# The last stage's feed-forward on rounded high and low halves, three products for each plain fp32 one, with the second matrix chunk by chunk

## The chip, the cores and the metric

The kernel runs on one core of a Trainium2 chip. The core has TensorE (PE, matrix products into PSUM), VectorE (DVE), ScalarE (ACT), GpSimd (POOL) and SyncE (SP, which here issues every DMA), each with its own instruction queue; they meet at semaphores. The metric is the device time of one execution in microseconds (us).

## What is computed

Only the part that the change touches is shown; `src` is the normalised input plus the mixture-of-experts attention that the earlier stages have made, and a second small causal attention is added at the end.

```python
src = _ln(src + src2, ln1_g, ln1_b)                 # src2: the attention with experts
src2 = jax.nn.relu(src @ W1 + b1) @ W2 + b2         # W1 (256, 1024), W2 (1024, 256)
ffn = _ln(src + src2, ln2_g, ln2_b)
out = x + attn(xn) @ WO + ffn                       # x (8, 512, 256), float32
```

## The kernel before

The batch has B = 8 sequences of 512 tokens with D = 256 features. A first stage normalises and turns all of them. A long loop over 64 steps (8 pairs of heads times 8 sequences, PAIRS = 64) makes projections, attention and the output mix of the experts; its steps are laid out by hand in eight slots for each engine (PE_FILL, ACT_FILL, DVE_FILL, POOL_FILL). Steps come in kinds: INNER in the loop, LAST for the 64th, TAIL for what trails behind it. In LAST and TAIL what remains of a step is mainly the mix: for each of 8 experts e VectorE makes uf (L1239), ScalarE rounds it to u_h (L1041), GpSimd makes the rest u_l = uf - u_h ("UL", L573), and TensorE multiplies wo_h by u_h and u_l and wo_l by u_h ("J", `mix`, L799).

This way of splitting an fp32 factor in a rounded high half and a low half (tiles of type float32r) and taking three products is used in the whole loop: GpSimd makes the halves of the weights from a staging tile (`halves`, L511 to L515: one add, a wait, one subtract), `split_wv` and `split_wo` once for each pair of heads.

The last stage works on one sequence b after another and is plain fp32. On TensorE (L908 to L922) one repetition is:

- `turn_y(b+1)`: 8 transposes of the next sequence (L880);
- `hidden(b, f)` for f = 0 to 7 (FC = 8 chunks of 128 hidden features): 2 matmuls of 512 columns each into bank f0 or f1 in turn (L897);
- `turn_s1(b+1)`: 8 transposes of the next normalised sequence (L888);
- `rows_of("z")`: hidden features times W2, 32 matmuls of 256 columns, after all of `hidden` (L905);
- `rows_of("w")`: 8 matmuls of 256 columns for the other attention's output (L905).

ScalarE takes each hidden chunk out of PSUM with one Relu (L1079), copies the turned s1 (L1068), and takes square roots for the norms (`roots`, L932). VectorE, in this order for each b: `first_norm(b+1)` (statistics L1102 and L1105, var L1107, the wait for the root, L1109 to L1114, L1116, then two multiplications over 128x1024, L1281 and L1282), `with_bias` (L1288), aT (L1300, L1301), the sum with z (L1306), the second norm (again L1102 to L1116), and the residual (L1312). GpSimd does three operations of 128x1024 for each sequence (L635, L637, L644), the last of which makes the tile that is stored. SyncE loads both matrices in one piece each (L477, L478) after the last of the mix's inputs is made, and TensorE waits for both (`c_in`, L910).

In a norm the root of `first_norm(b+1)` is taken by ScalarE at hidden chunk f = 4 (L1074), and that of the second norm of b right after the last chunk and the copies of s1 (L1082).

Of the kernel before, what the change touches and what calls it, by code (L numbers as in the profile page):

```python
# [6 lines left out]
B, S, D = 8, 512, 256  # L7
# [125 lines left out]
def build(nc, x, wqk, wv, wo, w_out, w1, w2, b1, rows, ident, ident_h, mask, rope, rank, out):  # L133
# [11 lines left out]
    with ExitStack() as ctx:  # L145
# [83 lines left out]
        s1T = probs[:, 1]  # L229
# [8 lines left out]
        den_all, rden_all = st[:, 1].rearrange("q (g s) -> q g s", g=2), st[:, 0, 0:S]  # L238
# [69 lines left out]
        s1_ready = sem("s1_ready")  # L308
        acc_ready = sem("acc_ready")
# [18 lines left out]
        def _(sp):  # L328
# [143 lines left out]
            for j in range(2):  # L472
                sp.wait_ge(wo_split[j], HP)
# [30 lines left out]
        def _(pool):  # L504
# [17 lines left out]
            def split_wv(p, j):  # L522
                pool.wait_ge(st_in[j], 32 * p + 16)
                halves(wv_h[:, j], wv_l[:, j], st[:, j].rearrange("q (k n) -> q k n", k=KC),
                       zero_hb[:, None, :].to_broadcast([NP, KC, S]), 5 * p + 2 + j, wv_split[j])

            def split_wo(p, j):
# [4 lines left out]
                       zero_hb[:, None, :].to_broadcast([NP, 2, S]), 5 * p + 4 + j, wo_split[j])  # L532
# [14 lines left out]
            def body(kind, it, p=None, wv_next=False, wo_now=False):  # L547
# [82 lines left out]
            body(TAIL, PAIRS - 1)  # L630

            pool.wait_ge(c_in, 64)
            for b in range(B):
                pool.wait_ge(acc_ready, b + 1)
                nc.gpsimd.tensor_tensor(acc, acc, rows_sb[:, 2:3, :].to_broadcast([NP, TT, D]), ALU.mult).then_inc(fin_step, 1)  # L635
                pool.wait_ge(fin_step, 2 * b + 1)
                nc.gpsimd.tensor_tensor(acc, acc, rows_sb[:, 3:4, :].to_broadcast([NP, TT, D]), ALU.add).then_inc(fin_step, 1)  # L637
                pool.wait_ge(fin_step, 2 * b + 2)
                pool.wait_ge(resid_ready, b + 1)
                if b > 0:  # L640
                    pool.wait_ge(out_stored, 16 * b)
                else:
                    pool.wait_ge(rden_out, 16)
                nc.gpsimd.tensor_tensor(fin, acc, x_c[b % 2], ALU.add).then_inc(fin_ready, 1)  # L644

        @block.tensor
        def _(pe):
# [243 lines left out]
            def hidden(b, f):  # L891
                if f == 0:
                    for k in range(KC):
                        pe.wait_ge(c_free[f"w{k}"], s1T_at(b) + 1)
                o = c_bank(f"f{f % 2}", b * (FC // 2) + f // 2)
# [14 lines left out]
            pe.wait_ge(c_in, 64)  # L910
# [14 lines left out]
        def _(act):  # L925
# [139 lines left out]
            def s1_out(b):  # L1065
                for k in range(KC):
                    act.wait_ge(c_full[f"w{k}"], s1T_at(b) + 1)
                    nc.scalar.activation(s1T[:, k, :], cbank[f"w{k}"][:], ACT.Copy).then_inc(c_free[f"w{k}"], 1)  # L1068
# [294 lines left out]
```

## Time and profile before

| | |
|---|---|
| median of 3 runs | 3404.74 us (3403.65 to 3405.85) |
| span of the profiled execution | 3401.4 us |
| its first to last instruction, clock granted to TensorE | 0.995 |
| TensorE, matmuls | 3233.1 us busy, 95% |
| VectorE | 2439.7 us, 72% |
| ScalarE | 1961.5 us, 58% |
| GpSimd | 1441.9 us, 42% |
| the last stage (from 3112 us on) | about 289 us of the span |

The span runs from the first to the last instruction; the time of a run is 3.3 us longer (3404.74 less 3401.4). The page cuts the span in 40 slices of 85 us, so the last stage is its last three and a half digits. In a row of the timeline the first number is the start from the span's start, the second how long the instruction ran in us, then come engine, line, operation, the tile written and those read; the bracket at the end says how long the engine had been idle and what released it. A matmul's record is longer than the distance to the next one, since they are pipelined: what one costs is read from start to start. A plain fp32 matmul leaves two records.

### The profile page before, as it was taken

To read this page: it belongs to the slowest core of one execution; us is meant where nothing else is said; L and a number is where in the kernel's file an instruction comes from. 1 tells how busy PE (TensorE), PEld (TensorE's weight loads), DVE (VectorE), ACT (ScalarE), POOL (GpSimd) and SP (SyncE) were. 2 spreads that over 40 slices of the span, in tenths; PEclk is the share of its full clock that TensorE was granted. 3 is DMA by queue.
4 is the path that set the end of the run, shared out by engine and by line. 5 is a ranking of instruction groups with operands and counts; after the bars stand their busy time and mean duration, and the time that the engine had idled before them with its cause. 6 is when DMAs were issued, how large, how long until landed. Compare 5 with 4: busy or idle time off the path is not lost.

```text
span 3401.4 us, 64468 instructions
## 1 busy us (share of the span) xinstructions
PE 3233.1 (95%) x18240; PEld 2378.9 (70%) x18240; DVE 2439.7 (72%) x4708; ACT 1961.5 (58%) x4509; POOL 1441.9 (42%) x1215
## 2 busy tenths in 40 slices
PE   1699999999999999999999999999999999997998
PEld 1577777777777777777777777777777777775765
DVE  6577777777777777777777777777777777775554
ACT  2466666656666666666666666666666666664121
POOL 4144355445443454345543554434534543442212
PEclk9999999999999999999999999999999999999999
DMA  5223333334233333233233332333332433333221
GB/s 165 76 71 87 95 90 85 77 76 109 76 84 87 84 98 81 75 100 96 69 87 76 96 98 77 76 104 81 84 87 68 114 81 75 84 75 110 72 83 62
DMA packets 115937, 295.18 MB, mean 87 GB/s; under 512 B 33856, under 2 KB 54592, under 8 KB 99264
## 3 DMA queue, kind: packets, MB, share of 16 engines
q1 hardware_dynamic: 115904, 294.78, 32.9%
q8 instruction: 15, 0.25, 0.0%
q14 instruction: 18, 0.15, 0.0%
HBM read 262.74 MB, written 31.98 MB: 87 GB/s over the span
## 4 chain that ended last, share of the span: by engine, by line
PE 85%; issue 6%; DVE 5%; ACT 3%; DMA 1%; POOL 0%; ACTq 0%; SPq 0%; DVEq 0%; POOLq 0%
PE bank L673 27%; PE bank L799 22%; PE bank L718 9%; PE bank L773 7%; PE bank L688 5%; PE bank L905 4%; PE bank L897 3%; PE bank L693 3%; PE bank L745 2%; PE bank L754 2%; ACT probs L957 2%; DVE uf L1239 1%; DVE oo L1232 1%; PE bank L694 1%; ACT pt_e L977 1%
## 5 line engine op out<-in xcount | busy, mean ns | idle before, releaser
L573 POOL TENSOR_TENSOR u_l<-uf,u_h 128x512 fp32r<-128x512 f32 x512 | 716.1, 1409 | 722.6 <-ACT u_h L1041 722.4
L1136 DVE TENSOR_REDUCE nmax<-bank 128x1 f32<-128x512 f32 (+3 forms) x1024 | 551.8, 579 | 305.0 <-PE bank L688 297.8
L673 PE MATMUL bank<-wv_h,xx 128*128 128x512 f32 x2048 | 755.0, 410 | 7.1 <-DVE vm L1157 7.1
L957 ACT ACTIVATE probs<-bank,nmax 128x512 f32<-128x512 f32 (+3 forms) x1024 | 590.7, 610 | 253.2 <-DVE nmax L1136 253.1
L1041 ACT ACTIVATE u_h<-uf 128x512 fp32r<-128x512 f32 x512 | 321.7, 632 | 696.9 <-DVE uf L1239 683.6
L673 PEld LDWEIGHTS bank<-wv_h,xx 128*128 128x128 f32 x2048 | 386.0, 188 | 155.8 <-issue 59.6
L718 PEld LDWEIGHTS bank<-ident_sb,probs 128*128 128x128 f32 x3328 | 388.3, 141 | 106.4 <-issue 51.3
L718 PE MATMUL bank<-ident_sb,probs 128*128 128x128 f32 x3328 | 451.3, 274 | 1.6 <-ACT stackT L1032 0.9
L569 POOL TENSOR_TENSOR v_sb<-v_next,zero_hb 128x512 f32<-128x512 f32 x64 | 74.2, 1160 | 891.9 <-PE bank L773 877.4
L799 PE MATMUL bank<-u_h,wo_h 128*128 128x512 f32 x1024 | 427.1, 417 | 5.0 <-ACT u_h L1041 3.2
L1239 DVE TENSOR_TENSOR uf<-oo,go 128x512 f32<-128x512 f32 x512 | 416.2, 823 | 8.8 <-POOL u_l L573 6.6
L799 PE MATMUL bank<-u_h,wo_l 128*128 128x512 f32 x1024 | 405.9, 396 | 0.0
L799 PE MATMUL bank<-u_l,wo_h 128*128 128x512 f32 x1024 | 405.0, 396 | 0.0
L673 PE MATMUL bank<-wv_l,xx 128*128 128x512 f32 x1024 | 404.8, 395 | 0.0
L1157 DVE TENSOR_TENSOR vm<-bank,gv 128x512 f32<-128x512 f32 x512 | 348.4, 681 | 41.6 <-PE bank L673 41.5
L1159 DVE TENSOR_REDUCE v_next<-vm 128x64 f32<-128x512 f32 x512 | 351.3, 686 | 17.6
L673 PE MATMUL bank<-wq_h,xx 128*128 128x384 f32 x1024 | 280.4, 344 | 12.8 <-DMA xx<-xs_d 12.7
L977 ACT ACTIVATE pt_e<-bank 128x512 f32<-128x512 f32 x512 | 276.1, 594 | 5.1 <-PE bank L718 0.5
L799 PEld LDWEIGHTS bank<-u_h,wo_h 128*128 128x128 f32 x1024 | 192.4, 188 | 66.5 <-issue 24.4
L773 PE MATMUL bank<-pt_e,v_sb 128*64 128x512 f32 x1024 | 233.8, 598 | 0.0
L1191 DVE TENSOR_SCALAR vm<-raw 128x128 f32<-128x128 f32 x64 | 14.5, 227 | 296.6 <-ACT raw L992 296.6
L799 PEld LDWEIGHTS bank<-u_h,wo_l 128*128 128x128 f32 x1024 | 192.5, 188 | 46.5
(141 smaller groups left out, 5164.2 us busy)
## 6 DMA issues: line engine op xcount, KB each, us to landing
go<-go_d SPq DMA_DIRECT2D x256, 512.0 KB, 6.5
xx<-xs_d SPq DMA_DIRECT2D x128, 512.0 KB, 3.5
oo<-scale_d SPq DMA_DIRECT2D x128, 128.0 KB, 2.9
a_d<-a_out SPq DMA_DIRECT2D x128, 128.0 KB, 2.3
pt_c<-in_x SPq DMA_DIRECT2D x16, 512.0 KB, 4.7
st<-in_wv SPq DMA_DIRECT2D x16, 512.0 KB, 5.8
st<-in_wo SPq DMA_DIRECT2D x16, 512.0 KB, 7.2
go_d<-go_turned SPq DMA_DIRECT2D x256, 8.0 KB
```

Of the source, the lines that this page charges most:

```text
L573: nc.gpsimd.tensor_tensor(u_l[:, e % 2], uf[:, e % 2], u_h.bitcast(f32)[:, e % 2], ALU.subtract).then_inc(ul_done, 1)
L673: last = nc.tensor.matmul(out, lhs, rhs, start=n == 1, stop=n == 3 * len(chunks))
L718: mm = nc.tensor.transpose(o[:, c * NP:(c + 1) * NP], probs[:, s % 2, j, c * NP:(c + 1) * NP], ident_sb[:])
L773: mm = nc.tensor.matmul(o[j * P:(j + 1) * P, :], v_sb[:, k, j, :], pt_e[:, j, k, :], start=k == 0, stop=k == TT - 1)
L799: mm = nc.tensor.matmul(ybank[i][:], w[:, e, c], u[:, e % 2], start=e == 0 and k == 0, stop=e == E - 1 and k == 2, skip_group_check=True)
L957: nc.scalar.activation(probs[:, s % 2, j, 0:w], sbank[j][:, 0:w], ACT.Exp, bias=nmax[:, 2 * s + j:2 * s + j + 1], **kw).then_inc(exp_done, 1)
L977: nc.scalar.activation(dst[:, j, 0:m, qt * NP:(qt + 1) * NP], tbank[j][:, 0:m * NP].rearrange("q (c m) -> q c m", m=NP), ACT.Copy).then_in ...
L1041: nc.scalar.activation(u_h[:, i % 2], uf[:, i % 2], ACT.Copy).then_inc(uh_done, 1)
L1136: nc.vector.tensor_reduce(nmax[:, 2 * s + j:2 * s + j + 1], sbank[j][:, 0:w], AX.X, ALU.max, negate=True).then_inc(nmax_ready, 1)
L1157: nc.vector.tensor_tensor(m, o[:].rearrange("q (c e) -> q c e", e=E), g, ALU.mult).then_inc(free, 1)
L1159: nc.vector.tensor_reduce(v_next[:, t, j, :], m, AX.X, ALU.add).then_inc(v_ready, 1)
L1239: nc.vector.tensor_tensor(uf[:, i % 2], oo[:, 0], go[:, i], ALU.mult).then_inc(u_ready, 1)
```

## The change

In the last stage both matrices, the turned s1 and the hidden features are kept as rounded high half and low half, and each fp32 product becomes three (high by high, high by low, low by high). In particular:

- The weights use the buffers of the loop: W1 goes through the staging tile into wv_h and wv_l, W2 into wo_h and wo_l. SyncE issues W1's two loads ahead of step LAST and W2's two behind it; GpSimd splits W1 inside LAST (after slots 2 and 4) and W2 behind TAIL.
- `hidden(b, f)` is 6 matmuls of 512 columns. `expand(b, f)` takes the place of `rows_of("z")`: 12 matmuls of 256 columns for one chunk f, which follow two chunks behind `hidden`; the last three come after `turn_s1(b+1)`.
- ScalarE takes each chunk out twice (plain, and rounded), then waits for its own second write before a small copy sets the bank free. `roots` for the second norm of the sequence before moves to chunk f = 1 of the next sequence.
- GpSimd makes the low half of each chunk (`hidden_rest`), and its three closing operations of the sequence before are placed behind chunks 2, 3 and 5.
- VectorE makes the low half of s1 (`s1_low`, two operations of 128x512 out of PSUM), behind aT.

```diff
-        w1_sb = go[:, 0:4].rearrange("q (k a) s -> q k (a s)", k=KC)
-        w2_sb = go[:, 4:8].rearrange("q a (c n) -> q (a c) n", n=D)
-        hT = pe8
+        hidden_f = [pe8[:, i] for i in range(4)]
+        hidden_h = [u_h[:, 0], u_h[:, 1], q_h[:], k_h[:]]
+        hidden_l = [u_l[:, 0], u_l[:, 1], q_l[:], k_l[:]]
...
+            for j in range(2):
+                sp.wait_ge(wo_split[j], HP)
+                sp.dma_start(st[:, j].rearrange("q (k n) -> q k n", k=KC), w1[:, :, j * F // 2:(j + 1) * F // 2]).then_inc(st_in[j], 16)
             body(HP - 1, B - 1, LAST, before=(HP - 1, B - 2))
+            for j in range(2):
+                sp.wait_ge(wv_split[j], HP + 1)
+                sp.dma_start(st[:, j].rearrange("q (a n) -> q a n", n=D), w2[:, j * FC // 2:(j + 1) * FC // 2, :]).then_inc(st_in[j], 16)
...
-            sp.wait_ge(u_ready, E * PAIRS)
-            sp.dma_start(w1_sb, w1).then_inc(c_in, 16)
-            sp.dma_start(w2_sb, w2).then_inc(c_in, 16)
...
+                    if kind == LAST and s in (2, 4):
+                        j = s // 2 - 1
+                        pool.wait_ge(w_full, w_at(INNER, PAIRS - 2, ("V", 5 + 2 * j))[2] + 1)
+                        split_wv(HP, j, 1)
...
+            for j in range(2):
+                pool.wait_ge(o_done, (PAIRS - 1) * E + (j + 1) * E // 2)
+                split_wo(HP, j, 3)
+
+            def hidden_rest(b, f):
+                n = b * FC + f
+                i = n % 4
+                pool.wait_ge(hidden_ready, n + 1)
+                if n >= 4:
+                    pool.wait_ge(z_step, n - 3)
+                nc.gpsimd.tensor_tensor(hidden_l[i], hidden_f[i], hidden_h[i].bitcast(f32), ALU.subtract).then_inc(hidden_low, 1)
...
+                for f in range(FC):
+                    hidden_rest(b, f)
+                    if b > 0 and f in (2, 3, 5):
+                        finish(b - 1, (2, 3, 5).index(f))
...
                 o = c_bank(f"f{f % 2}", b * (FC // 2) + f // 2)
-                for k in range(KC):
-                    mm = nc.tensor.matmul(o[:], w1_sb[:, k, f * NP:(f + 1) * NP], s1T[:, k, :], start=k == 0, stop=k == KC - 1)
-                mm.then_inc(c_full[f"f{f % 2}"], 1)
+                j, c = f // (FC // 2), slice(f % (FC // 2) * NP, (f % (FC // 2) + 1) * NP)
+                three(o[:], [(wv_h[:, j, k, c], wv_l[:, j, k, c], s1T[:, 0, k, :], s1T[:, 1, k, :]) for k in range(KC)]).then_inc(c_full[f"f{f % 2}"], 1)
+
+            def expand(b, f):
...
+                pe.wait_ge(hidden_low, n + 1)
+                hi, lo = hidden_h[n % 4], hidden_l[n % 4]
+                for t in range(TT):
+                    o = cbank[f"z{t // 2}"][:, (t % 2) * D:(t % 2 + 1) * D]
+                    c = slice(t * NP, (t + 1) * NP)
+                    for i, (lhs, w) in enumerate(((hi[:, c], wo_h), (hi[:, c], wo_l), (lo[:, c], wo_h))):
+                        mm = nc.tensor.matmul(o, lhs, w[:, f, :], start=f == 0 and i == 0 and t % 2 == 0, stop=f == FC - 1 and i == 2,
...
                 for f in range(FC):
                     hidden(b, f)
+                    if f > 1 and f < FC - 1:
+                        expand(b, f - 2)
                 if b + 1 < B:
                     turn_s1(b + 1)
-                for i in range(2):
-                    pe.wait_ge(c_free[f"f{i}"], (b + 1) * (FC // 2))
-                rows_of("z", b, hT, w2_sb, FC)
+                for f in range(FC - 3, FC):
+                    expand(b, f)
...
+                nc.scalar.activation(hidden_f[i], o[:], ACT.Relu, bias=b1_sb[:, f:f + 1])
+                nc.scalar.activation(hidden_h[i], o[:], ACT.Relu, bias=b1_sb[:, f:f + 1]).then_inc(hidden_ready, 1)
+                act.wait_ge(hidden_ready, n + 1)
+                nc.scalar.activation(primer[:, 1:2], ident_sb[0:1, 0:1], ACT.Copy).then_inc(c_free[f"f{f % 2}"], 1)
...
+                    if f == 1 and b > 0:
+                        roots(B + 2 * b)
                     if f == FC // 2 and b + 1 < B:
                         roots(B + 2 * b + 1)
...
+            def s1_low(b):
+                for k in range(KC):
+                    dve.wait_ge(s1h_ready, KC * b + k + 1)
+                    nc.vector.tensor_tensor(s1T[:, 1, k, :], cbank[f"w{k}"][:], s1T[:, 0, k, :].bitcast(f32), ALU.subtract).then_inc(c_free[f"w{k}"], 1)
...
+                if b + 1 < B:
+                    s1_low(b + 1)
                 if b > 0:
                     dve.wait_ge(fin_ready, b)
```

## Rows read from the trace of the kernel before

**Rows 1.** The page: TensorE's busy tenths in 40 slices.

```profile
PE   1699999999999999999999999999999999997998
```

**Rows 2.** Chain of waits in order of time, one repetition of the last stage.

```profile
3290.86 0.87 PE bank L880 x8
3291.74 13.73 PE bank L897 x32
...
3306.37 17.43 PE bank L905 x80
3323.80 0.87 PE bank L880 x8
```

**Rows 3.** The same repetition: length, then busy us of PE, PEld, DVE, ACT, POOL; clock.

```profile
3290.90:3323.80 32.90, 32.90 (x130) 22.84 (x129) 19.16 (x50) 6.77 (x12) 7.06 (x3) 1.00 0.25 80
```

**Rows 4.** Timeline of TensorE, split matmuls of 512 and 384 columns.

```profile
1501.62 0.39 PE L673 MATMUL bank<-wv_h,xx 128*128 128x512 f32 x1
1501.85 0.39 PE L673 MATMUL bank<-wv_l,xx 128*128 128x512 f32 x1
...
1521.33 0.33 PE L673 MATMUL bank<-wq_l,xx 128*128 128x384 f32 x1
...
1521.85 0.33 PE L673 MATMUL bank<-wq_l,xx 128*128 128x384 f32 x1
```

**Rows 5.** Timeline of TensorE's weight loads, the first two after an idle time.

```profile
3100.36 0.19 PEld L799 LDWEIGHTS bank<-u_h,wo_h 128*128 128x128 f32 x1 [0.71 <-issue]
3100.47 0.19 PEld L799 LDWEIGHTS bank<-u_l,wo_h 128*128 128x128 f32 x1
```

**Rows 6.** Timeline of ScalarE, first stage: the first reading of two banks in turn.

```profile
23.38 0.60 ACT L941 ACTIVATE y_sb<-bank 128x512 f32<-128x512 f32 x1 [7.36 <-PE bank L659]
...
24.75 0.57 ACT L941 ACTIVATE y_sb<-bank 128x512 f32<-128x512 f32 x1
```

**Rows 7.** Timelines of VectorE and GpSimd, small VectorE operations beside GpSimd's.

```profile
27.57 2.04 DVE L1112 TENSOR_TENSOR root<-root,rstd 128x4 f32<-128x4 f32 x1
...
27.48 2.12 POOL L513 TENSOR_TENSOR wv_h<-st,zero_hb 128x1024 fp32r<-128x1024 f32 x1
29.68 2.34 POOL L515 TENSOR_TENSOR wv_l<-st,wv_h 128x1024 fp32r<-128x1024 f32 x1
...
3257.94 0.16 DVE L1112 TENSOR_TENSOR root<-root,rstd 128x4 f32<-128x4 f32 x1
...
3263.13 1.69 DVE L1107 TENSOR_SCALAR var<-mv 128x4 f32<-128x4 f32 x1
...
3262.44 2.35 POOL L637 TENSOR_TENSOR pt_c<-pt_c,raw 128x1024 f32<-128x1024 f32 x1
```

**Rows 8.** Timeline of VectorE, landmarks of one repetition of the last stage.

```profile
3254.51 0.69 DVE L1306 TENSOR_TENSOR pt_c<-bank,pt_c 128x512 f32<-128x512 f32 x1 [6.03 <-PE bank L905]
...
3261.26 1.42 DVE L1102 BATCH_NORM_STATS2 stats<-bank 128x6 f32<-128x256 f32 x4
...
3266.51 0.18 DVE L1109 RECIPROCAL rstd<-root 128x4 f32<-128x4 f32 x1 [1.70 <-ACT root L932]
...
3274.45 1.22 DVE L1301 TENSOR_TENSOR uf<-uf,oo 128x1024 f32<-128x1024 f32 x1
```

**Rows 9.** Groups by line and form, GpSimd: a low half of 128x512 (mean ns second).

```profile
L537 POOL TENSOR_TENSOR q_l<-y_sb,q_h 128x512 fp32r<-128x512 f32 x4 | 5.1, 1265 | 27.6 <-ACT primer L945 27.6
```

**Rows 10.** Timelines: GpSimd in steps LAST and TAIL, VectorE behind TAIL.

```profile
3069.85 2.70 POOL L573 TENSOR_TENSOR u_l<-uf,u_h 128x512 fp32r<-128x512 f32 x2 [3.17 <-ACT u_h L1041]
3075.03 2.52 POOL L573 TENSOR_TENSOR u_l<-uf,u_h 128x512 fp32r<-128x512 f32 x2 [2.48 <-ACT u_h L1041]
...
3082.62 1.30 POOL L573 TENSOR_TENSOR u_l<-uf,u_h 128x512 fp32r<-128x512 f32 x1 [2.48 <-ACT u_h L1041]
...
3106.72 1.29 POOL L573 TENSOR_TENSOR u_l<-uf,u_h 128x512 fp32r<-128x512 f32 x1 [0.70 <-ACT u_h L1041]
...
3111.05 0.55 DVE L1292 TENSOR_TENSOR st<-st 128x384 f32<-128x384 f32 x1
```

More of the change, by code:

```diff
@@ L308, in build @@
         s1_ready = sem("s1_ready")
+        s1h_ready = sem("s1h_ready")
+        hidden_ready = sem("hidden_ready")
+        hidden_low = sem("hidden_low")
+        z_step = sem("z_step")
         acc_ready = sem("acc_ready")
@@ L531, in split_wo @@
                        st[:, j].rearrange("q (a n) -> q a n", a=2),
-                       zero_hb[:, None, :].to_broadcast([NP, 2, S]), 5 * p + 4 + j, wo_split[j])
+                       zero_hb[:, None, :].to_broadcast([NP, 2, S]), 5 * p + step + j, wo_split[j])
             def split_x(b):
@@ new lines, in hidden_rest, with finish @@
+            def hidden_rest(b, f):
[5 more added lines that the diff above has]
+                nc.gpsimd.tensor_tensor(hidden_l[i], hidden_f[i], hidden_h[i].bitcast(f32), ALU.subtract).then_inc(hidden_low, 1)
+            def finish(b, step):
+                if step == 0:
+                    pool.wait_ge(acc_ready, b + 1)
+                    nc.gpsimd.tensor_tensor(acc, acc, rows_sb[:, 2:3, :].to_broadcast([NP, TT, D]), ALU.mult).then_inc(fin_step, 1)
+                elif step == 1:
+                    pool.wait_ge(fin_step, 2 * b + 1)
+                    nc.gpsimd.tensor_tensor(acc, acc, rows_sb[:, 3:4, :].to_broadcast([NP, TT, D]), ALU.add).then_inc(fin_step, 1)
+                else:
+                    pool.wait_ge(fin_step, 2 * b + 2)
+                    pool.wait_ge(resid_ready, b + 1)
+                    if b > 0:
+                        pool.wait_ge(out_stored, 16 * b)
+                    nc.gpsimd.tensor_tensor(fin, acc, x_c[b % 2], ALU.add).then_inc(fin_ready, 1)
@@ L646, in _ @@
+            pool.wait_ge(c_in, 32)
+            for b in range(B):
+                for f in range(FC):
+                    hidden_rest(b, f)
+                    if b > 0 and f in (2, 3, 5):
+                        finish(b - 1, (2, 3, 5).index(f))
+            for step in range(3):
+                finish(B - 1, step)
         @block.tensor
@@ L894, in hidden @@
                         pe.wait_ge(c_free[f"w{k}"], s1T_at(b) + 1)
+                    if b == 0:
+                        for j in range(2):
+                            pe.wait_ge(wv_split[j], HP + 1)
                 o = c_bank(f"f{f % 2}", b * (FC // 2) + f // 2)
-                for k in range(KC):
-                    mm = nc.tensor.matmul(o[:], w1_sb[:, k, f * NP:(f + 1) * NP], s1T[:, k, :], start=k == 0, stop=k == KC - 1)
-                mm.then_inc(c_full[f"f{f % 2}"], 1)
+                j, c = f // (FC // 2), slice(f % (FC // 2) * NP, (f % (FC // 2) + 1) * NP)
+                three(o[:], [(wv_h[:, j, k, c], wv_l[:, j, k, c], s1T[:, 0, k, :], s1T[:, 1, k, :]) for k in range(KC)]).then_inc(c_full[f"f{f % 2}"], 1)
+            def expand(b, f):
+                if f == 0:
+                    c_bank("z0", b)
+                    c_bank("z1", b)
+                if b == 0 and f % (FC // 2) == 0:
+                    pe.wait_ge(wo_split[f // (FC // 2)], HP + 1)
+                n = b * FC + f
+                pe.wait_ge(hidden_low, n + 1)
[5 more added lines that the diff above has]
+                        mm = nc.tensor.matmul(o, lhs, w[:, f, :], start=f == 0 and i == 0 and t % 2 == 0, stop=f == FC - 1 and i == 2,
+                                              skip_group_check=True)
+                    if f == FC - 1 and t == 1:
+                        mm.then_inc(c_full["z0"], 1)
+                mm.then_inc(z_step, 1)
             def rows_of(name, at, lhs, w, chunks):
@@ L909, in _ @@
             turn_s1(0)
-            pe.wait_ge(c_in, 64)
+            pe.wait_ge(c_in, 32)
             for b in range(B):
@@ L1073, in _ @@
                 for f in range(FC):
+                    if f == 1 and b > 0:
+                        roots(B + 2 * b)
                     if f == FC // 2 and b + 1 < B:
                         roots(B + 2 * b + 1)
-                    if f == 0 and b > 0:
-                        act.wait_ge(c_full["z1"], b)
-                    act.wait_ge(c_full[f"f{f % 2}"], b * (FC // 2) + f // 2 + 1)
-                    nc.scalar.activation(hT[:, f, :], cbank[f"f{f % 2}"][:], ACT.Relu, bias=b1_sb[:, f:f + 1]).then_inc(c_free[f"f{f % 2}"], 1)
+                    hidden_out(b, f)
                 if b + 1 < B:
                     s1_out(b + 1)
-                roots(B + 2 * b + (2 if b + 1 < B else 1))
+            roots(B + 2 * B - 1)
         @block.vector
@@ L1294, in _ @@
             first_norm(0, B)
+            s1_low(0)
             for b in range(B):
@@ L1304, in _ @@
                 for i in range(2):
-                    dve.wait_ge(c_full[f"z{i}"], b + 1)
+                    if i == 0:
+                        dve.wait_ge(c_full["z0"], b + 1)
+                    else:
+                        dve.wait_ge(z_step, (b + 1) * FC)
                     made(nc.vector.tensor_tensor(acc[:, 2 * i:2 * i + 2, :], cbank[f"z{i}"][:].rearrange("q (t d) -> q t d", t=2), s1[b % 2][:, 2 * i:2 * i + 2, :], ALU.add))
```

34 lines of the change are left out of this document (14 added, 20 removed).

## Prediction

> **What bounds the kernel now.** I read the page first: TensorE is busy nine tenths or more in nearly every slice, most of the last stage included [rows 1]. Then the chain of waits in order of time, for the stage that changes: it stays on TensorE without a gap, and the pattern repeats every 3323.80 - 3290.86 = 32.94 us: 0.87 for `turn_y`, 13.73 for `hidden`, 0.90 for `turn_s1` (what is left up to 3306.37), 17.43 for z and w together [rows 2]. The same stretch by windows shows TensorE full, at a granted clock of 1.00, and VectorE 19.2, ScalarE 6.8, GpSimd 7.1 of 32.9 us [rows 3]. So the plain fp32 products are the bound now, and TensorE work taken away counts until another engine ends last. The reader should look at how far the others are from it, and at what they wait for; the busy sums alone mislead here.
>
> **TensorE's side.** Removed: 16 hidden matmuls (13.73 us, 0.858 each) and 32 of z. The 17.43 us are 40 matmuls of 256 columns, 0.436 each with the change of banks; z's 32 are 13.9 and w's 8 are 3.5. Added for each sequence:
>
> - 48 split matmuls of 512 columns. The loop has the same kind: start to start 1501.85 - 1501.62 = 0.23 [rows 4]; 48 x 0.233 = 11.2.
> - 96 split matmuls of 256 columns. The trace has no such form. Three of 384 columns take 1521.85 - 1521.33 = 0.52, 0.174 each [rows 4]. The straight line through 512 and 384 gives 0.115 at 256. A weight load could hold them up: its record is 0.19 long, but at the head of a chain, where nothing else is in the way, the second load starts 3100.47 - 3100.36 = 0.11 behind the first [rows 5], so loads can follow at 0.11. Bounds: 0.11 and the whole record, 0.19. I take 0.117, by the line, which is just above the pace of the loads: 96 x 0.117 = 11.2.
>
> With the turns (0.87 and 0.9) and w (3.5) TensorE needs 27.7, plus 0.3 at `hidden(2)`, which waits for ScalarE to free bank f0 (below): 28.0, that is 4.9 less than now. If TensorE stayed the bound, that would be some 37 us over the stage.
>
> **What ends last instead.** The change gives the others work and, above all, order.
>
> ScalarE: two readings and a small copy for each chunk. The first stage has this pattern, two readings of a bank, a wait, a small copy, and takes 24.75 - 23.38 = 1.37 for the whole [rows 6]; some 1.4 here. TensorE spends 1.4 on a chunk, 2.8 with `expand`. That fits, but the bank of chunk 0 is free only about 3.1 + 0.9 into the repetition, hence the 0.3.
>
> GpSimd: 8 low halves at 1.27 [rows 9] are 10.2, and the three closing operations of about 2.4 are 7.1 [rows 3]: 17.3 where it had 7.1. All closing operations and six of the halves fall between about 8 and 23 us of a repetition, so it works there almost without a break.
>
> VectorE: beside a GpSimd operation its small operations on SBUF don't run. L1112, 0.16 alone, took 2.04 and ended at 29.61, where GpSimd's L513 ends at 29.60; L1107, as small, took 1.69 and ended at 3264.82, GpSimd's L637 at 3264.79 [rows 7]. GpSimd's next operation starts in between, so a chain of such operations loses one GpSimd operation at each link. Operations with an input in PSUM show no such delay.
>
> Now one repetition, from `turn_y` at 0. The pieces of VectorE's chain add up to its landmarks: from the sum with z to the next statistics 6.75, of which 1.9 for statistics and var, 0.3 for the root, 0.9 for L1109 to L1114, 1.3 for L1116, 1.3 for the residual; from L1109 to the end of L1301 9.2, a wait of 0.3 in it [rows 8].
>
> - Root of the second norm of the sequence before. Its var is ready at about 0.3, but ScalarE takes the root only at chunk 1, behind chunk 0: hidden(0) ends at 2.3, drained 2.5, two readings and copy to 3.9, root 4.1. VectorE stands for 3.8. Before, the root was taken at once.
> - L1109 to L1114, 0.9 alone, with two waits for low halves (0.6 and 1.0): 6.8. Four L1116, 1.3: 8.1 (sum ready for GpSimd). Residual, 1.3: 9.4.
> - `first_norm` of the next sequence: statistics 1.9, var with 0.5 of wait, 12.0; root 12.2.
> - L1109 to L1114: behind a closing operation 1.7, behind two low halves 1.1 and 0.8: 16.9. Four L1116 from PSUM 1.9: 18.9. L1281 and L1282 (1.22 each) in turn with low halves, 1.0 of wait: 22.4, s1 is ready.
> - TensorE came to `turn_s1` at 0.87 + 0.3 + 11.2 + 7.0 (5 of the 8 expands) = 19.4 and waits 3.1. From 22.5: turn 0.9, three expands 4.2, w 3.5: 31.1 to 31.2. aT and s1_low (about 5 us of VectorE) lie beside the turn and the expands, and end with them.
>
> So a repetition is 31.2, not 28.0: VectorE's chain with two roots and the waits for GpSimd takes 3.1 of the 4.9 back. Over the stage: six repetitions at -1.75 are -10.5; the first has no closing operations and no second norm before it, so it keeps the gain of TensorE but pays s1_low ahead of `hidden` (0.9): -3.9; the last has no `first_norm`, but is held up by GpSimd's queue for about 2: -3.5. Behind the last z the chain (sum, norm, three GpSimd operations, store) is the same. Sum -17.9.
>
> On this a rule of the Trainium skill bears, page "SBUF — State Buffer", section "Who interferes with whom": a VectorE instruction with two SBUF inputs, or in a two-port mode, contends with a GpSimd instruction that reads SBUF, and whichever issued second blocks in full until the other is done. The rows agree for L1112 and L1107. The page speaks against this change, for it gives GpSimd 10 us more in the very window of the norms; without it the sum would be that of the first rival. The page adds that tensor_scalar can be in such a mode too; for L1116 on SBUF that is the second rival.
>
> **Ahead of the stage.** W1's split, 2.12 + 2.34 with a gap of 0.08 for each half [rows 7], goes into step LAST on GpSimd's queue. Queued behind it are the low halves of u, for which TensorE's mix waits. First half: starts when the fourth u_l is done, 3072.55, and runs to 3077.1; the fifth u_l started at 3075.03 [rows 10], so the mix is 2.1 to 2.5 late. Second half: after the sixth, now at 3079.7, to 3084.3; the seventh then ends at 3085.6 and the eighth at 3086.9, which ended at 3082.62 + 1.30 = 3083.9 [rows 10]. So I take the mixes there as 3.3 late (3.0 by the eighth, the rest for TensorE's turn on the seventh), and I see nothing behind them in LAST or TAIL with slack to give that back. W2's split, 9.1 us behind TAIL's last u_l (3106.72 + 1.29 = 3108.0), covers VectorE's L1292 at 3111.05 [rows 10], two SBUF inputs, which waits for the second operation to end, 1.5; the reciprocal, the norm and the turn hang on it. It is done before the first chunk's low half is due. Sum +4.8. Bounds: 2 (LAST absorbs most) and 8 (another wait in the norm).
>
> The loads: W1's two stand ahead of LAST's, W2's two behind its, and they wait for splits done long before or at 3084.3; what SyncE has queued behind them (rows, w_out, the last of the causal attention, x, the denominators) is wanted after 3108.0 only. GpSimd waits for W2 behind TAIL, over 20 us later. The two loads of 1 MB behind the last mix go away; TensorE's wait for them was over before its first hidden chunk, which waited for the norm. I cost both at nothing; if a load of 0.5 MB came late, it would be 6 us once.
>
> **Sum.** -17.9 + 4.8 = -13.1. Profiled span 3401.4 - 13.1 = 3388.3; with the 3.3 around it, 3391.6, say 3392. The median of before is 3404.74, which is 3401.4 + 3.3, so span and time move together.
>
> **The rivals.**
>
> - TensorE stays the bound. For it: VectorE's own work is only about 21 us of a repetition, and a slightly different phase of GpSimd's operations would spare several waits. Against it: the root at chunk 1 and the rows of L1112 and L1107. Then 28.0 for a repetition, stage -37, sum -32: 3372.
> - GpSimd holds VectorE up further: L1116 on SBUF waits as well, four in each second norm. Nothing in the trace shows it beside GpSimd; its 0.32 us from start to start for 256 elements is the pace of an operation that isn't in a fast mode. Then 32.2 for a repetition, -1.0 less for each of seven: -6, with the upper bound ahead of the stage -2: 3399 to 3403.
> - Slower: the weight load is the pace of the 256-column matmuls. 96 weight loads for each sequence are twice those of z before, and each serves half the columns of one in `hidden`. At the record's 0.19 `expand` takes 18.2, a repetition 35.1, the stage +17 and all +22: 3427. It decides from about 0.16 on, where a repetition with the costs ahead of the stage comes to what it was. The 0.11 between the first two loads of a chain speaks against it.
> - The change doesn't do what it says, the split products run as slow as plain ones. That would be hundreds of us; 0.23 for 512 columns in the loop excludes it as good as surely.
>
> **How the numbers follow.** Forecast 0.50 (3384 to 3399), TensorE-bound 0.17, held up further 0.22, weight loads 0.06, others 0.05. A measurement of this kernel can tell about 0.2%, 6.8 us, from no change: faster means under 3398, slower over 3411.5. Faster: 0.45 of the forecast, 0.17, 0.06 of the third case: 0.68. Slower: 0.06, 0.02 of the third, 0.03 of the others: 0.11. Same: the rest, 0.21. The range reaches from the first rival's 3371 to the upper bound of the second, 3406; what is left out is under 0.2.
>
> **What would show it.** In the profile after: matmuls of `expand` 0.117 apart; a wait of TensorE's `turn_s1` (L888's successor) for VectorE's L1282 of about 3 us in each repetition; repetitions of 31.2; VectorE's small operations at 0.6 to 1.8 us beside GpSimd's; GpSimd near full in the middle of a repetition; ScalarE's root of the second norm some 4 us behind its var; TensorE 3.3 us late at the end of LAST. Wrong would make it: a repetition of 28 without the wait; expands over 0.13 apart; or a TensorE idle for so long that its clock falls.

## The result and the profile after

| | before | after |
|---|---|---|
| median | 3405.13 us (3403.65 to 3406.82, 5 runs) | 3418.23 us (3417.27 to 3420.49, 5 runs) |
| span of the profiled execution | 3401.4 us | 3416.4 us |
| granted clock, whole span | 0.995 | 0.988 |
| GpSimd busy | 1441.9 us | 1545.9 us |

The ratio is 1.004, with a 95% interval from 1.0027 to 1.0053: the kernel became 13 us slower, where 13 us faster was forecast. The predicted range (3371 to 3406) does not hold the time.

The page of the kernel after, TensorE's busy tenths and its clock, shows where: only the last digits differ from [rows 1].

```profile
PE   1699999999999999999999999999999999997887
...
PEclk9999999999999999999999999999999999999988
```

The chain of waits of one repetition of the last stage (start, us, what), the counterpart of [rows 2]. In the changed file L909 is `turn_y`, L702 the three products of `hidden`, L1130 the rounded reading of ScalarE, L983 the root, L1174 to L1177 the old L1111 to L1114, L1179 the old L1116, L1344 and L1345 the old L1281 and L1282, L917 `turn_s1`, L944 `expand`, L955 w.

```profile
3230.82 0.87 PE bank L909 x8
3231.70 1.40 PE bank L702 x6
...
3233.81 0.59 ACT u_h L1130
...
3234.97 0.82 DVE root L1174
...
3236.01 1.26 DVE root L1176
...
3244.10 1.89 DVE root L1174
...
3246.01 1.22 DVE root L1175
3247.25 1.23 DVE root L1176
3248.51 2.31 DVE rstd L1177
3250.85 1.90 DVE probs L1179 x4
...
3254.35 1.24 DVE probs L1345
...
3255.63 1.97 PE bank L917 x8
3257.60 6.04 PE bank L944 x36
3263.64 3.45 PE bank L955 x16
3267.10 0.87 PE bank L909 x8
```

The repetition takes 3267.10 - 3230.82 = 36.28 us; the six of this kind take 36.2, 35.3, 36.3, 35.3, 36.3 and 35.3, on average 35.8, against 32.94 before and 31.2 forecast. The chain is on TensorE only at the two ends. Between them it is mostly on VectorE, at operations on 128x4 elements that need 0.16 to 0.18 us when alone and take 0.8 to 2.3 us here.

The same repetition by windows (length, then busy us of PE, PEld, DVE, ACT, POOL; granted clock), the counterpart of [rows 3]:

```profile
3230.82:3267.10 36.28, 30.77 (x179) 27.52 (x177) 27.81 (x52) 12.91 (x28) 17.22 (x11) 0.91 0.22 73
3250.00:3255.00 5.00, 0.34 (x2) 0.00 (x0) 4.88 (x9) 1.47 (x3) 3.23 (x3) 0.96 0.62 194
3255.00:3260.00 5.00, 4.37 (x21) 4.37 (x22) 4.93 (x6) 1.20 (x2) 0.00 (x0) 0.50 0.06 19
```

TensorE stands nearly still from 3250 to 3255, and when it starts again, the granted clock is 0.50, that is 1.2 GHz instead of 2.4. So the wait is paid twice: once as a wait, and once as `turn_s1` at 1.97 us instead of 0.87 and 36 matmuls of `expand` at 6.04 us.

The two profiled spans differ by 15.0 us, the medians by 13.1; what lies outside the span is 1.8 us in this profiled execution and 3.3 in that of before. Where the 15.0 us are, from matching starts in the two chains:

| stretch | before | after | difference | forecast |
|---|---|---|---|---|
| up to the attention of step LAST | 3058.1 | 3056.6 | -1.5 | 0 |
| LAST, attention to attention | 29.4 | 35.3 | +5.9 | +3.3 |
| TAIL, up to the old L1292 | 23.7 | 23.7 | 0.0 | 0 |
| from there to the first `turn_s1` | 11.5 | 12.9 | +1.4 | +1.5 |
| first repetition | 36.5 | 30.9 | -5.6 | -3.9 |
| six repetitions | 197.6 | 214.7 | +17.1 | -10.5 |
| last repetition | 28.7 | 25.6 | -3.1 | -3.5 |
| behind the last z | 16.0 | 16.7 | +0.7 | 0 |

The first row is not the change's: over the profiles of this study the attention of LAST starts anywhere from 3054.9 to 3061.6 us. The six repetitions are the miss, 27.6 us against their forecast.

### The profile page after: what moved, and what is told of

It is laid out like the page before. It is cut to its first block, busy times and chain, and to the rows that moved or that the text cites. A ratio compares the mean times of both kernels' runs of the same rounds, so it can differ in the third digit from the quotient of the medians.

```text
span 3416.4 us, 65572 instructions
## 1 busy us (share of the span) xinstructions
PE 3209.8 (94%) x18624; PEld 2410.1 (71%) x18624; DVE 2509.8 (73%) x4724; ACT 2010.9 (59%) x4637; POOL 1545.9 (45%) x1287
## 4 chain that ended last, share of the span: by engine, by line
PE 80%; DVE 9%; issue 6%; ACT 3%; POOL 1%; DMA 1%; ACTq 0%; SPq 0%; DVEq 0%; POOLq 0%
PE bank L702 28%; PE bank L828 21%; PE bank L747 9%; PE bank L802 7%; PE bank L717 5%; PE bank L722 3%; PE bank L774 2%; PE bank L783 2%; DVE uf L1302 2%; ACT probs L1008 2%; PE bank L944 1%; DVE oo L1295 1%; PE bank L723 1%; DVE pt_c L1179 1%; PE bank L955 1%
## 5 line engine op out<-in xcount | busy, mean ns | idle before, releaser
L702 PE MATMUL bank<-wv_h,xx 128*128 128x512 f32 x2048 | 754.8, 410 | 7.1 <-DVE vm L1220 7.1
L702 PEld LDWEIGHTS bank<-wv_h,xx 128*128 128x128 f32 x2048 | 386.2, 189 | 155.3 <-issue 59.6
L702 PE MATMUL bank<-wv_l,xx 128*128 128x512 f32 x1024 | 404.4, 395 | 0.0
L702 PE MATMUL bank<-wq_h,xx 128*128 128x384 f32 x1024 | 279.8, 344 | 11.7 <-DMA xx<-xs_d 11.7
L828 PEld LDWEIGHTS bank<-u_h,wo_h 128*128 128x128 f32 x1024 | 192.7, 188 | 70.5 <-issue 25.6
```

Source lines behind the costliest of these rows:

```text
L702: last = nc.tensor.matmul(out, lhs, rhs, start=n == 1, stop=n == 3 * len(chunks))
L828: mm = nc.tensor.matmul(ybank[i][:], w[:, e, c], u[:, e % 2], start=e == 0 and k == 0, stop=e == E - 1 and k == 2, skip_group_check=True)
```

## The experiments

**The two theories at the outset.** After reading the trace of the kernel after, I held that the middle of a repetition is a chain of small VectorE operations, each held until the GpSimd operation beside it ends, and that the wait which this gives TensorE also costs clock. The timelines of the two engines (start, length, engine, line, operation, tiles) show the pairs:

```profile
3244.10 1.87 DVE L1174 TENSOR_TENSOR root<-var,rstd 128x4 f32<-128x4 f32 x1
3246.01 1.21 DVE L1175 TENSOR_TENSOR root<-root,rstd 128x4 f32<-128x4 f32 x1
3247.25 1.22 DVE L1176 TENSOR_SCALAR root<-root 128x4 f32<-128x4 f32 x1
3248.51 2.30 DVE L1177 TENSOR_TENSOR rstd<-rstd,root 128x4 f32<-128x4 f32 x1
...
3243.53 2.42 POOL L658 TENSOR_TENSOR pt_c<-pt_c,raw 128x1024 f32<-128x1024 f32 x1
3245.91 2.54 POOL L650 TENSOR_TENSOR u_l<-pt_e,u_h 128x512 fp32r<-128x512 f32 x2
3248.40 2.39 POOL L664 TENSOR_TENSOR st<-pt_c 128x1024 f32<-128x1024 f32 x1
```

L1174 ends at 3245.97, GpSimd's L658 at 3245.95; L1175 ends at 3247.22, in the middle of the two low halves (3247.18); L1176 at 3248.47, where the second low half ends (3248.45); L1177 at 3250.81, L664 at 3250.79. Four operations that need 0.7 us take 6.6. The rivals to it: the late root, the clock by itself, and the work ahead of the stage.

**e1: the root one chunk earlier.** ScalarE takes the root of the second norm ahead of chunk 0 of the next sequence; in the kernel after it takes it ahead of chunk 1, so behind chunk 0.

```diff
-                    if f == 1 and b > 0:
+                    if f == 0 and b > 0:
                         roots(B + 2 * b)
```

> One edit of the changed kernel: ScalarE takes the root of the second norm ahead of chunk 0 of the next sequence, not behind it. Theory A (VectorE's chain of two norms sets when s1 is ready, and the late root is 3.4 us of it): VectorE gets this root at about 0.6 us of a repetition, not 3.9; s1 is ready at about 22.4, not 24.8; TensorE waits some 3 us ahead of the turn, its granted clock doesn't fall, and a repetition takes about 31.2 where it took 35.8 on average. The whole is 25 to 30 us faster than the changed kernel, about 3390. Rival B (GpSimd's operations alone set VectorE's pace; it would have waited for them anyway): s1 comes at 24 or later, TensorE still waits over 4.5 us and goes cold, at most 5 us gained. Rival C (the loss sits ahead of the stage): no change.

Measured: 3398.54 us (10 runs), ratio 0.9982 (0.9972 to 0.9991), some 20 us under the kernel after, less than the 25 to 30 expected: the waits are shorter, but the clock still fell in three of the six repetitions. The `turn_y`s are 32.7, 32.5, 32.7, 31.2 and 31.2 us apart, where 31.2 was expected for all. In windows two successive repetitions stand beside each other, and the difference between them is the clock:

```profile
3224.45:3257.14 32.69, 29.70 (x179) 26.49 (x177) 27.30 (x53) 13.02 (x28) 19.11 (x11) 0.95 0.25 81
3257.14:3288.33 31.19, 28.20 (x179) 25.00 (x177) 26.78 (x51) 12.82 (x27) 19.11 (x11) 1.00 0.26 85
```

The place of one 0.2 us operation of ScalarE is worth 20 us. But s1 is ready 22.3 us into the repetition (22.4 expected), TensorE still waits 2.78 us for L1345, and the small operations of `first_norm` are still held (L1175 1.20, L1176 2.33, L1177 1.21). The timeline of VectorE shows a second wait in front of them:

```profile
3267.13 0.18 DVE L1172 RECIPROCAL rstd<-root 128x4 f32<-128x4 f32 x1 [3.64 <-ACT root L983]
...
3268.96 2.33 DVE L1176 TENSOR_SCALAR root<-root 128x4 f32<-128x4 f32 x1
```

The root of `first_norm` is still taken ahead of chunk 4, and VectorE, now earlier, stands 3.64 us for it, where it stood 0.27 in the kernel after. So about half of what the early root of the second norm gives is lost at the other root: var is ready 6.3 us into the repetition instead of 12.8, its root is used at 10.0 instead of 13.1. In e6 below this wait is still 1.79 us; no run moves that root.

**e2: without two of the three closing operations.** GpSimd's multiplication by ln2_g and addition of ln2_b are left out, so that the output lacks them; the last closing operation, the sum with x, stays behind chunk 5.

```diff
-                if step == 0:
-                    pool.wait_ge(acc_ready, b + 1)
-                    nc.gpsimd.tensor_tensor(acc, acc, rows_sb[:, 2:3, :].to_broadcast([NP, TT, D]), ALU.mult).then_inc(fin_step, 1)
-                elif step == 1:
-                    pool.wait_ge(fin_step, 2 * b + 1)
-                    nc.gpsimd.tensor_tensor(acc, acc, rows_sb[:, 3:4, :].to_broadcast([NP, TT, D]), ALU.add).then_inc(fin_step, 1)
```

> One edit of the changed kernel: GpSimd's first two closing operations of each sequence (times ln2_g, plus ln2_b, 128x1024 each) are left out, so the output lacks them. Theory A with the shared port as I read it (VectorE's small operations on SBUF wait for whole GpSimd operations, and those behind a closing operation lose 1.7 to 2.3 us each): L1114's counterpart ends at about 14, not 20, of a repetition, s1 is ready at about 21.2, a repetition is some 31, no cold clock; with one closing operation less at the end as well (two of 2.3 behind the last norm), 35 us faster than the changed kernel. Rival (VectorE's chain is long by itself, the waits for GpSimd would only move to the low halves): s1 at 24 or later, a repetition over 34, only the 5 us at the end gained.

Measured: 3385.29 us, ratio 0.9943 (0.9927 to 0.996), 33 us under the kernel after where 35 were expected. 4.7 us of the gain on the kernel after are those two operations behind the last sequence, where nothing hides them (2.34 and 2.33 in its chain); the rest is in the repetitions, now 30.9 us. The chain of waits of one shows the first norm's operations free (compare the four above):

```profile
3236.78 0.19 DVE rstd L1166
3236.99 0.17 DVE root L1168
3237.18 0.17 DVE root L1169
3237.38 0.18 DVE root L1170
3237.58 0.17 DVE rstd L1171
```

s1 is ready 21.1 us into the repetition (21.2 expected). The root is still ahead of chunk 1 here, as in the kernel after. So holding by GpSimd is a cause by itself.

**e3: TensorE kept busy while it waits.** 24 matmuls whose result is overwritten stand ahead of the wait of `turn_s1`.

```diff
             def turn_s1(b):
...
+                if b > 0:
+                    o = c_bank("w0", s1T_at(b))
+                    for i in range(24):
+                        nc.tensor.matmul(o[:], wv_h[:, 0, 0, 0:NP], wv_h[:, 0, 0, :], start=True, stop=True)
```

> One edit of the changed kernel: TensorE runs 24 matmuls of 512 columns (about 5.5 us) whose result is overwritten, ahead of its wait for s1, in each repetition but the first. Theory A (the wait of 5.7 us is VectorE's; on top of it TensorE's clock falls to 1.2 GHz and the turn and the first expands behind it cost 2 to 3 us more): s1 is ready at the same 24.8, the turn takes 0.9 instead of 1.97 and the 36 matmuls of expand 4.3 instead of 5.1 to 6.1; a repetition is 33.5, about 13 us faster in all. Rival B (those matmuls are slow for another reason, such as contention with the copies of s1): they stay at 5 to 6 us, no gain, or a loss if the added matmuls outlast the wait.

Measured: 3415.54 us (3410.99 to 3417.02), ratio 1.003 (1.0017 to 1.0042), against 1.004 (1.0027 to 1.0053) for the kernel after: the intervals overlap, and the gain of 2.7 us between medians is not resolved; 13 had been expected. The profiled execution is the fastest of the six (3410.99), so its span shows more than the median does. What a repetition does can be read in it all the same. The chain of waits of one repetition:

```profile
3251.35 5.44 PE bank L916 x24
3256.78 1.01 PE bank L921 x8
3257.80 4.31 PE bank L948 x36
```

And the window behind the wait, for which the kernel after had a clock of 0.50, now has 1.00:

```profile
3255.00:3260.00 5.00, 5.00 (x36) 4.42 (x36) 4.90 (x6) 1.09 (x2) 0.00 (x0) 1.00 0.28 91
```

The turn takes 1.01 instead of 1.97, the 36 matmuls of `expand` 4.31 instead of 6.04, and repetitions are 33.7 instead of 35.8 us. The six gain 12.3 us; the first, in which TensorE had not waited, pays 5.4 for the added matmuls. That makes -6.9; with the 0.4 us that the stage starts earlier in this profile it is the difference between the spans, 3409.1 - 3416.4 = -7.3. s1 is ready at the same 24.8. So the clock is worth 2.1 us of a repetition, and the chain on VectorE the rest: with a full clock and the same chain a repetition is still longer than before.

**e4: W1 split later.** Both halves of W1 are split behind slot 7 of LAST instead of slots 2 and 4.

```diff
-                    if kind == LAST and s in (2, 4):
-                        j = s // 2 - 1
-                        pool.wait_ge(w_full, w_at(INNER, PAIRS - 2, ("V", 5 + 2 * j))[2] + 1)
-                        split_wv(HP, j, 1)
+                    if kind == LAST and s == SLOTS - 1:
+                        for j in range(2):
+                            pool.wait_ge(w_full, w_at(INNER, PAIRS - 2, ("V", 5 + 2 * j))[2] + 1)
+                            split_wv(HP, j, 1)
```

> One edit of the changed kernel: both halves of W1 are split on GpSimd behind slot 7 of step LAST, not behind slots 2 and 4. From the traces, LAST (from its first attention product to TAIL's) took 29.4 us before and 35.3 after. Theory A (the split delays the low halves of u behind it and VectorE's products beside it by 5.9 us in LAST): LAST is 29.4 again, at most 1 us comes back at TAIL's start, and the whole is 4 to 6 us faster. Rival (those delays only move to TAIL, whose first low half then stands behind 9 us of splits): within 2 us of the changed kernel, or slower.

Measured: 3417.99 us (3414.49 to 3419.75), ratio 1.0039 (1.0024 to 1.0053), no difference from the kernel after that could be told, where 4 to 6 us were expected. In the profile LAST goes from 35.3 back to 29.4 us, the length before the change, and TAIL gives back 2.1 of it (25.9 instead of 23.7 to L1360), where at most 1 was expected. Why LAST had paid 5.9 and not 3.3 is to be read in the chain of waits of the kernel after, with GpSimd's timeline under it:

```profile
3073.57 4.44 DVE uf L1302 x2
...
3072.54 2.16 POOL L518 TENSOR_TENSOR wv_h<-st,zero_hb 128x1024 fp32r<-128x1024 f32 x1
3074.77 2.67 POOL L520 TENSOR_TENSOR wv_l<-st,wv_h 128x1024 fp32r<-128x1024 f32 x1
```

Two products uf (two SBUF inputs), 1.28 us for both where nothing runs beside them, took 4.44 us beside the first split. I had looked only at what stands behind the split on GpSimd's own queue.

**e5: root and split together.** The edits of e1 and e4 in one kernel. In the texts expected from here on, the root "behind chunk 0" means the place of e1, ahead of chunk 0, and "behind chunk 1" the place in the kernel after, ahead of chunk 1.

> The square root of the second norm behind chunk 0 instead of 1, and both W1 halves split behind slot 7 of step LAST instead of slots 2 and 4. Theory (the split makes LAST longer because VectorE's uf products stand behind it; the root's place sets how VectorE's small operations of the first norm meet the closing steps): the two gains add, since they lie in different stages: repetitions of 31.2 to 32.7 us as with the root alone, LAST at 29.4 us, GpSimd behind TAIL some 2 us later; together 3.8 us under the root alone, about 3394 us. Rival (the W1 split placed late takes back in TAIL all that LAST gains, as the medians of the split alone would have it): 3398 us, as the root alone.

Measured: 3395.87 us (3392.68 to 3398.85), ratio 0.9974 (0.9964 to 0.9985), repetitions 31.2, one of them 32.7. That is 2.7 us under the median of e1, whose interval (0.9972 to 0.9991) overlaps; the forecast of 3.8 us more is neither confirmed nor excluded.

**e6: the closing operations moved.** On top of e5 GpSimd's three closing operations stand behind chunks 2, 2 and 7 instead of 2, 3 and 5. Nothing is left out.

```diff
-                    if b > 0 and f in (2, 3, 5):
-                        finish(b - 1, (2, 3, 5).index(f))
+                    for step in range(3):
+                        if b > 0 and f == (2, 2, 7)[step]:
+                            finish(b - 1, step)
```

> The kernel with root and split moved, and GpSimd's three closing operations behind chunks 2, 2 and 7 instead of 2, 3 and 5: the work is the same, only its place. Theory (VectorE's small operations of the norm, each of which waits for the end of the GpSimd operation beside it, carry s1 past the moment at which TensorE wants it, and the wait also costs the clock): between the second closing step and chunk 7 VectorE meets only the short low halves, s1 is ready before TensorE has finished chunk 7 and its interleaved part, no wait at the transposes of s1, granted clock stays full, repetitions of 28.9 to 29.5 us, in all 3380 to 3384 us. Rival (GpSimd as a whole is what is late: the third closing step behind chunk 7 holds back the low half of the next sequence's first chunks and the tile for VectorE's residual): repetitions of 31 to 32 us, no gain on the kernel without the move, 3393 us or more.

Measured: 3377.97 us (3376.46 to 3378.98), ratio 0.992 (0.9907 to 0.9934): 27 us faster than before, 40 faster than the kernel after, and faster than the e2 kernel that leaves work out. The `turn_y`s are 29.0 us apart in all five that follow the first. One repetition by windows:

```profile
3215.65:3244.64 28.99, 28.43 (x178) 24.98 (x177) 25.05 (x53) 12.89 (x28) 19.17 (x11) 1.00 0.28 92
```

GpSimd is busy 19.2 of 29.0 us, a larger share than in the kernel after, and VectorE 25.1, yet TensorE is full and its clock too. The timeline of VectorE (its line numbers are one higher) shows the same operations as above:

```profile
3225.96 0.35 DVE L1175 TENSOR_TENSOR root<-var,rstd 128x4 f32<-128x4 f32 x1
3226.34 0.16 DVE L1176 TENSOR_TENSOR root<-root,rstd 128x4 f32<-128x4 f32 x1
3226.53 2.26 DVE L1177 TENSOR_SCALAR root<-root 128x4 f32<-128x4 f32 x1
3228.83 1.19 DVE L1178 TENSOR_TENSOR rstd<-rstd,root 128x4 f32<-128x4 f32 x1
```

They take 4.0 us instead of 6.6 and begin 3.0 us earlier in the repetition, and s1 is ready 3234.84 - 3215.65 = 19.2 us into it, where it was 24.8; TensorE's `turn_s1` at 3235.78 follows its last matmul with no idle time on record. The total came out 2 us under the expected 3380, the repetitions at 29.0 in the expected 28.9 to 29.5.

**e7: closing operations behind chunks 2, 7 and 7.** The same edit with `(2, 7, 7)`.

> As the last, with the closing operations behind chunks 2, 7 and 7: VectorE meets one closing step in the norm instead of two, but twice as much GpSimd work stands behind chunk 7. Theory of the small VectorE operations: s1 early as well, repetitions of 29 to 30 us, 3382 to 3388 us. Rival (GpSimd's lateness): two closing steps behind chunk 7, some 4.8 us, come straight ahead of the next sequence's low halves, so this is clearly slower than with one there: 3395 us or more.

Measured: 3379.06 us (3378.5 to 3380.0), ratio 0.9923 (0.991 to 0.9937), repetitions 28.4 to 29.4 us: the same as e6, and better than I expected. Two closing operations behind chunk 7 do not hold up the next sequence: GpSimd's timeline has 4.99 us of idle time ahead of its next low half. The rival, that GpSimd as a whole is what is late, is out.

**e8: the closing operations alone.** The edit of e6 on the kernel after: root behind chunk 1, split in slots 2 and 4.

> The kernel after, with nothing changed but the places of GpSimd's closing operations: behind chunks 2, 2 and 7 (root behind chunk 1, W1 split in slots 2 and 4, as in the kernel after). Theory (the closing operations beside VectorE's small ones are the cause): nearly the whole gain comes from this edit alone; the later root makes VectorE's chain some 2.8 us later than with all three edits, where TensorE had 0.8 us to spare, so repetitions of 29.5 to 31 us and a total of 3385 to 3396 us. Rival (the root's place is what counts, the places of the closing operations help only beside it): repetitions above 33 us, 3405 us or more.

Measured: 3407.88 us (3404.17 to 3409.71), ratio 1.0013 (1.0004 to 1.0022), repetitions of 32.8 to 33.1 us. I had expected 3385 to 3396, and the rival was right: with the late root this move brings some 10 us, with the early one (e1 to e9, e5 to e6) 16 to 18 (by the ratios, each to before on its own chip, 9 and 16 to 18). The timelines of GpSimd and TensorE, with what ended the idle time ahead of each, show how the two hang together:

```profile
3239.37 2.41 POOL L655 TENSOR_TENSOR pt_c<-pt_c,raw 128x1024 f32<-128x1024 f32 x1 [0.88 <-DVE pt_c L1180]
3241.86 2.40 POOL L658 TENSOR_TENSOR pt_c<-pt_c,raw 128x1024 f32<-128x1024 f32 x1
3244.21 1.27 POOL L650 TENSOR_TENSOR k_l<-pt_e,k_h 128x512 fp32r<-128x512 f32 x1
...
3245.53 0.39 PE L945 MATMUL bank<-wo_h,k_h 128*128 128x256 f32 x1 [1.28 <-POOL k_l L650]
...
3252.57 1.09 PE L918 MATMUL bank<-ident_sb,probs 128*128 128x128 f32 x8 [1.17 <-DVE probs L1346]
...
3259.71 3.69 PE L956 MATMUL bank<-vm,uf 128*128 128x256 f32 x16 [1.76 <-DVE xx L1357]
```

A late root makes the sum late, GpSimd stands 0.88 us for it, both closing operations then come ahead of the low half of chunk 3, and TensorE waits 1.28 us for that low half; the rest comes at `turn_s1` and at w. I had carried the later root over to VectorE's chain alone, and not to GpSimd, which waits for that chain.

**e9: root and closing operations, split left in LAST.**

> Root behind chunk 0 and closing operations behind chunks 2, 2 and 7, with the W1 split left in slots 2 and 4 of LAST as in the kernel after. Theory (splitting in LAST costs VectorE's products there, and 2.1 us of it come back in TAIL): repetitions of 29.0 us as with all three edits, LAST at 35.3 instead of 29.4 us, 3.8 us over them: about 3382 us. Rival (the place of the split makes no difference to the time, as the medians of the split alone had it): 3378 us.

Measured: 3380.13 us (3376.46 to 3382.91), ratio 0.9935 (0.9922 to 0.9949), repetitions 29.0. LAST takes 33.7 and the way to L1361 23.7 us, together 57.4, where e6 has 29.3 and 25.8, together 55.1. So in these two profiles the late split gains 2.3 us. The other profiles agree on the sign: LAST and TAIL together take 57.4 to 60.0 us in the six with the early split and 55.1 to 56.7 in the four with the late one, 53.1 before. In the whole it is not resolved. The three pairs of medians that differ in it alone (kernel after and e4, e1 and e5, e9 and e6) all have the late split ahead, by 0.2, 2.7 and 2.2 us, and each with overlapping intervals; e9 ran on another chip than e6, and by the ratios their gap is 5. What the place of the split is worth in the whole stays open between nothing and some 5 us.

## Why the prediction was wrong

**Right: TensorE's price.** The matmuls of 256 columns, which the trace of before did not have, were put at 0.117 us. In e3, 12 take 1.41 to 1.43 us with TensorE in the chain, 0.118 each, and six products of 512 columns 1.37 to 1.40 us, 0.23 each; in the kernel after they come at the same distance at full clock:

```profile
3262.64 0.28 PE L944 MATMUL bank<-wo_h,k_l 128*128 128x256 f32 x1
3262.76 0.28 PE L944 MATMUL bank<-wo_h,k_h 128*128 128x256 f32 x1
3262.88 0.28 PE L944 MATMUL bank<-wo_l,k_h 128*128 128x256 f32 x1
```

TensorE's sum of 28.0 us for a repetition is 28.4 busy in e6. The rival of the weight loads, which needed 0.16 or more for each, is out, though the kernel is slower, as it would have been by that rival; a sign alone would have taken the wrong cause for the right one.

**Right: the root, the end, L1292.** The late root is done 3.9 us into the repetition (forecast 4.1). The last repetition is 3.1 us shorter (3.5), and L1292, now L1360, took 1.83 instead of 0.48 (+1.4 against +1.5). The first repetition gained 5.6 instead of 3.9, a term that was too small: the 0.9 for `s1_low` ahead of `hidden` cost nothing, since it lay beside `turn_y`, and the first `hidden` before had taken 14.42 instead of 13.73.

**Wrong, first step: which VectorE operations GpSimd holds.** I gave L1109 to L1114 "two waits" in the second norm and three in the first, no more than there are operations with two inputs in SBUF. L1113 has one, a tensor_scalar on 128x4; it was held as well (L1176: 1.25 us in the second norm, 1.22 in the first, 0.17 when free). In the second norm this changed nothing, since L1112 and L1114 were free and the two waits came to 0.6 and 1.1 as forecast; in the first norm it made four waits of three. And of the four L1116 with input in SBUF one was held, here in the kernel after and then in e6's second norm:

```profile
3237.49 2.36 DVE L1179 TENSOR_SCALAR pt_c<-pt_c,mv,rstd 128x256 f32<-128x256 f32 x4
...
3218.33 1.38 DVE L1180 TENSOR_SCALAR pt_c<-pt_c,mv,rstd 128x256 f32<-128x256 f32 x4
```

For this I had made a rival of its own with 0.22, and argued against it from the pace of the free operation. The pace, 1.38 us for four, is what I had read; being held did not depend on it. The rows on record spoke against me: L1107, one of the two held operations of [rows 7], is a tensor_scalar with one input. I had read it "as small" instead of by its form. (L1113 itself took 0.17 us in the trace of before at 29.65, but it started 0.03 us ahead of GpSimd's next operation, so that row did not clear it.) The Trainium skill, page "SBUF — State Buffer", section "Who interferes with whom", names tensor_scalar as an operation that can run in a two-port mode and then contends; L1176 and L1179 on SBUF agree with it, and L1179 with its input in PSUM, 1.90 us for four in the repetitions shown, was not held. Which mode these operations ran in no run here shows.

**What it cascaded to.** One more link made the chain reach the next, longer GpSimd operation. The first norm's four operations lost 1.7 + 1.05 + 1.05 + 2.1 = 5.9 us, where I had 1.7 + 1.1 + 0.8 = 3.6; var came at 12.8 instead of 12.0; L1281 and L1282 lost 0.3 instead of 1.0. 22.4 + 2.3 + 0.8 - 0.7 = 24.8, and the trace has s1 ready at 24.8. (The pieces listed in the prediction come to some 0.7 us less than its 22.4; 0.2 is missing at each of 6.8, 12.0 and 16.9. And the upper end of its range, 3406, is put down to a rival whose own figures end at 3403. Neither is what failed.)

**Wrong, second step: TensorE's wait priced at its length.** I forecast a wait of 3.1 us and named a fall of the clock only among the things that would make the forecast wrong, with no price. The wait was 5.3 us on record, and behind it the turn and three `expand`s took 1.97 + 6.04 = 8.0 instead of the 5.3 us of e3. That is 2.7 us in this repetition, and 2.1 on average by e3. With it, 31.2 + 2.4 + 2.7 = 36.3, the measured 36.28.

Behind waits of 2.8 to 2.9 us, in e1 and e5, the clock fell in four repetitions and not in the other eight (0.95 and 1.00 above). What decides between the two these runs do not show.

**Wrong, third step: the split in LAST.** +5.9 instead of +3.3 (+4.4 to +5.9 over the six profiles with the split in this place), since VectorE's products uf, two SBUF inputs, were held beside it. For VectorE in the last stage I had applied the rule, and for VectorE in LAST I had not asked.

**What bounds the kernel after**, then, is not how much work GpSimd has but when. e6 does all of it in 29.0 us for a repetition, close to the first rival's 28.0, which I had at 0.17. I had argued for it from "a slightly different phase of GpSimd's operations", and left it at that, without working out which order would give that phase.

## What to carry to other kernels

Before counting on a faster engine, go through the chain of small operations that will end last one by one and ask of each by its form (inputs in SBUF or PSUM, tensor_scalar included) whether another engine can hold it; each link that is held costs what is left of the other engine's operation, here up to 2.3 us, not its own 0.2 us. Then place the long operations of that other engine where no such chain runs, and take the result of the chain as early as it is there: here the two moves together brought 3418 to about 3380 us with no work removed, one alone 3399 or 3408. Where TensorE's wait grows, price what the wait costs behind it too, in clock: 2.1 us for a repetition here.

## What the runs showed of the hardware

- VectorE's tensor_scalar on 128x4 with one SBUF input is held until GpSimd's operation ends, up to 2.33 us (L1176 in e1) instead of 0.17. On 128x256 from SBUF, four took 2.36 us beside GpSimd and 1.38 without. The same operation with its input in PSUM, beside GpSimd's low halves, took 1.90 us for four, as in the kernel before.
- The granted clock was 0.50 in the window behind a wait of 5.3 us, and a whole repetition with such a wait had 0.91; with TensorE kept at work through the wait it stayed at 1.00 (e3).
- Matmuls on rounded halves follow each other at 0.118 us for 256 columns and 0.23 for 512, each with its own weight load. A load's record is 0.19 us long, so that length did not set the pace; whether the loads, which start 0.12 apart as well, set it at 256 columns no run separates.
